# A four-layer graph network on one core: GpSimd waits for its own gathers ahead of every twelfth group

## The chip, the core and the metric

The program runs on one core of a Trainium2 chip. The metric is the device time of one execution in microseconds (us), the median over runs. The engines are TensorE (PE, with its weight loads PEld), VectorE (DVE), ScalarE (ACT), GpSimd (POOL) and SyncE (SP), each with a queue of its own; they meet on semaphores. Stores and plain loads are issued by SP, gathers by GpSimd.

## What is computed

Four graph layers in a row over the same graph of 3125 nodes and 100000 edges that are sorted by their target `dst`, each behind a layer norm and a rectifier, each added to its input `x`. The change touches the attention over incoming edges, which layer 1 does twice and layer 2 once:

```python
def _transformer_conv(x, src, dst, ...):       # layer 1, twice
    q = (x @ qw + qb).reshape(N, HEADS, CH)    # 8 heads of 16
    k = (x @ kw + kb).reshape(N, HEADS, CH)
    v = (x @ vw + vb).reshape(N, HEADS, CH)
    alpha = jnp.sum(q[dst] * k[src], axis=-1) * SCALE
    m = segment_max(alpha, dst); a = exp(alpha - m[dst])
    a = a / segment_sum(a, dst)[dst]
    out = segment_sum(v[src] * a[:, :, None], dst)
    return out + x @ sw + sb
# layer 2: the same with a bias by edge type, then projection, norms and a small MLP
# layer 0: two convolutions with the mean over edges; layer 3: two with the maximum over edges
```

## The kernel before

The edges lie in 128 partitions, 784 consecutive edges each, so the running sums and maxima over the edges of one target are scans along the free axis. Passes 0 and 1 (sums) go by another method. Passes 2, 3 and 4 are the attention passes, passes 5 and 6 the maxima; each walks the 784 steps in 56 groups of `GROUP` = 14 steps. The passes run one after the other, as each needs the node rows that the one before leaves.

For one group of an attention pass GpSimd issues 14 indirect DMAs. Each gathers, for the 128 edges of one step (one in each partition), the row of the source node out of `table[k]` in HBM: key and value, 256 numbers of 4 bytes, so 131 KB a gather. They land in one of `RING` = 3 slots of the buffer `ring` (which lies in `arena`) and count on the semaphore of the slot, `s_land` ("rows_landed"). Ahead of a group g from 3 on GpSimd waits on `s_att`, until VectorE has read the values of group g - 3 out of the slot. In groups 5, 12, 19, 26, ... (g mod 7 is 5) GpSimd first issues one more indirect DMA, `fetch_window`, for the queries of seven later groups.

VectorE works on group g in two parts. `part_a`: L1085 (queries of late edges), L1113 (moves the window on), then a wait until the 14 gathers of the group have landed, and L1092 (query times key), L1094 (sum to scores), L1097, L1099, L1101 (running maximum and exponents). `part_b`, one group behind: L1131, L1136 (value times weight), L1140 (the running sum, 4.15 us). ScalarE does the exponentials, spreads the queries, and lays the finished rows out in `outs` (L1579, L1582), which SP stores to HBM (L2183, 1.0 MB a group). At the end of a pass GpSimd joins the partitions' first rows (a gather of the head row, a scatter of it at L2405 and a wait for that scatter) and gathers the rows of the nodes.

All gathers are recorded at L2316, in the helper `fetch`. Within GpSimd's queue the instructions go in the order in which they are written in `run_pass`; nothing reorders them.

Of the kernel before, what the change touches and what calls it, by code (L numbers as in the profile page):

```python
# [48 lines left out]
RING = 3  # L49
# [9 lines left out]
PICKED = (GROUPS - PICK_FROM) * MAKE  # L59
TURN_AT = 12  # L60
SHARE = 7
QROWS = SHARE + 1
SPANS = GROUPS // SHARE
MOVES = SHARE - 1
STEPS = GROUP * GROUPS
# [113 lines left out]
def gnn_kernel(nc, A):  # L179
# [10 lines left out]
    with ctx:  # L190
# [3 lines left out]
        def sem(name):  # L194
            return ctx.enter_context(nc.semaphore(name))
# [19 lines left out]
        WINDOW_AT = RING * GROUP * 2 * D  # L215
        arena = sb("arena", [P, WINDOW_AT + 2 * QROWS * D])
        ring = arena[:, 0:RING * GROUP * 2 * D].rearrange("p (s j w) -> p s j w", s=RING, j=GROUP)

        window = arena[:, WINDOW_AT:WINDOW_AT + 2 * QROWS * D].rearrange("p (s r f) -> p s r f", s=2, r=QROWS)

# [250 lines left out]
        s_land = [sem(f"rows_landed{s}") for s in range(RING)]  # L471
# [113 lines left out]
        def landed(k, g):  # L585
            return land_count[k, g]
# [4 lines left out]
        def window_moved(k, g):  # L591

            return att_number(k) * (MOVES * SPANS) + g // SHARE * MOVES + g % SHARE

# [26 lines left out]
        def after_b(k, g, i):  # L621
            if isinstance(g, int) and g == GROUPS - 2:
                return (GROUPS - 1) * A_STEPS[k] + 1 + B_STEPS * g + att_base[k] + i
            na = GROUPS if isinstance(g, int) and g == GROUPS - 1 else g + 2
            return na * A_STEPS[k] + B_STEPS * g + att_base[k] + i
# [43 lines left out]
        def _(v):  # L669
# [436 lines left out]
            def move_on(k, g):  # L1106

                if g % SHARE == 0:
                    return
                rows3, left, n = window[:, g // SHARE % 2, :, :], QROWS - g % SHARE, window_moved(k, g)  # L1110
                if n > 1:
# [1182 lines left out]
        def _(pool):  # L2294
# [41 lines left out]
            def run_pass(k):  # L2336
# [21 lines left out]
                with pool.Else():  # L2358
                    fetch_window(k, 0)
                    for g in range(GROUPS):  # L2360
                        s, first = g % RING, g * GROUP
                        if g >= RING:
                            pool.wait_ge(s_att, after_b(k, g - RING, 2))
                        if g % SHARE == SHARE - 2 and g + 2 < GROUPS:
                            fetch_window(k, (g + 2) // SHARE)
                        for j in range(GROUP):
                            fetch(ring[:, s, j, :], table[k], src_i[:, first + j:first + j + 1], s_land[s])
# [111 lines left out]
```

## Time and profile before

| what | us |
|---|---|
| median of 3 runs | 5820.93 |
| lowest and highest run | 5820.36, 5821.15 |
| span of the profiled execution | 6562.2 |
| attention pass 2, first gather to last L1092 | 780 to 1865 |
| attention pass 3 | 1960 to 3045 |
| attention pass 4 | 3154 to 4242 |
| maximum passes 5 and 6, first to last scan of each | 4408 to 5416, 5502 to 6498 |

The profiled execution is the only one of which the trace tells; no time of it besides its span is given, and that span is 741 us above the median of the runs. All moments in this text are us from the start of that span. In the timeline a row is one instruction with its start, its duration, and in brackets how long its engine stood idle before it and what ended that; "issue" means that the profile shows nothing that it waited for. The duration of an indirect DMA on POOL is the time in which GpSimd makes it, and not the time until its data have landed.

### The profile page before, as it was taken

The page shows a single profiled execution, that of the slowest core. Times are in us where ns is not written, and L with a number is a line of the kernel's source. Part 1 is how long each engine was busy: PE and PEld are TensorE (multiplying, and loading weights), DVE is VectorE, ACT ScalarE, POOL GpSimd, SP SyncE. Part 2 cuts the span into 40 slices and gives each one's busy share as a digit, 9 for nine tenths or more (in the row PEclk, how much of TensorE's full clock was granted, in tenths as well). Part 3 has the DMA queues.
Part 4 walks back from the last instruction along what each step waited for, and adds up shares of the span by engine and source line. Part 5 has one row for each costly group of instructions (what it writes and reads, how often), then busy time and mean ns, then how long its engine had stood idle before and what let it go on. Part 6 is the DMA issues. An engine that isn't in the chain of part 4 may idle for free.

```text
span 6562.2 us, 44574 instructions
## 1 busy us (share of the span) xinstructions
PE 2310.6 (35%) x14635; PEld 1387.8 (21%) x14635; DVE 4507.3 (69%) x5353; ACT 2519.0 (38%) x3136; POOL 3944.3 (60%) x3878
## 2 busy tenths in 40 slices
PE   4988400000020000000100000046877783778886
PEld 2775300000000000000000000023444441444443
DVE  7978587777767777776787777764655653656654
ACT  2330144444424444443344444433444442444443
POOL 1001377777747777775677777656665555566664
PEclk8998755555555555555555555567888895889887
DMA  2233354444434444443454444412333322333332
GB/s 64 83 136 135 110 163 152 153 147 146 152 117 151 157 148 147 152 148 113 134 160 152 147 148 146 142 46 86 102 110 101 101 95 73 102 110 109 98 103 84
DMA packets 257146, 807.72 MB, mean 123 GB/s; under 512 B 72026, under 2 KB 108938, under 8 KB 253123
## 3 DMA queue, kind: packets, MB, share of 16 engines
q0 software_dynamic: 162688, 416.67, 22.2%
q1 hardware_dynamic: 94279, 389.14, 16.2%
q8 instruction: 54, 0.88, 0.1%
q14 instruction: 125, 1.02, 0.0%
HBM read 473.23 MB, written 332.30 MB: 123 GB/s over the span
## 4 chain that ended last, share of the span: by engine, by line
POOL 38%; PE 26%; issue 22%; DVE 8%; ACT 2%; another core or an unknown queue 2%; DMA 1%; SPq 0%; DVEq 0%; POOLq 0%; ACTq 0%
POOL arena L2316 38%; PE pair_ps L1864 20%; PE pair_ps L1966 3%; DVE outs L917 2%; ACT outs L1702 1%; PE banks_ps L1830 1%; PE banks_ps L1942 1%; DVE outs L995 1%; PE pair_ps L1873 0%; DVE bn_st L700 0%; DVE H L1048 0%; ACT arena L1680 0%; PE pair_ps L1982 0%; PE banks_ps L1807 0%
## 5 line engine op out<-in xcount | busy, mean ns | idle before, releaser
L2316 POOL DMA_INDIRECT arena<-table,src_i x3596 | 3684.6, 1025 | 1549.8 <-issue 1134.4
L1842 PE MATMUL pair_ps<-ident,tails 128*128 128x128 f32 x9 | 2.7, 439 | 3331.7 <-DVE tails L1246 3331.7
L1864 PE MATMUL pair_ps<-bias,arena 128*128 128x384 bf16 x4050 | 803.9, 348 | 279.9 <-issue 239.9
L1092 DVE TENSOR_TENSOR pair_ps<-pair_ps,arena 128x1792 f32<-128x1792 f32 x168 | 341.5, 2033 | 764.7 <-DMA arena<-table,src_i 589.1
L1864 PE MATMUL pair_ps<-work,arena 128*128 128x384 bf16 x4050 | 760.5, 338 | 206.4 <-issue 204.8
L995 DVE TENSOR_TENSOR_SCAN outs<-arena,banks_ps 128x1920 f32<-128x1920 f32 x112 | 465.2, 4153 | 494.3 <-ACT banks_ps L1688 446.2
L1842 PEld LDWEIGHTS pair_ps<-ident,tails 128*128 128x128 f32 x9 | 1.5, 213 | 3334.0 <-DVE tails L1246 3334.0
L1140 DVE TENSOR_TENSOR_SCAN work<-work,banks_ps 128x1920 f32<-128x1920 f32 x168 | 697.7, 4153 | 5.8
L1562 ACT ACTIVATE LD<-DE 128x112 f32<-128x112 f32 x168 | 49.8, 296 | 1440.9 <-issue 571.3
L1864 PEld LDWEIGHTS pair_ps<-bias,arena 128*128 128x128 bf16 x4050 | 406.9, 102 | 661.6 <-issue 452.8
L1582 ACT COPY outs<-work 128x1792 f32<-128x1792 f32 x171 | 541.0, 3165 | 0.0
L1702 ACT COPY outs<-outs 128x1792 f32<-128x1792 f32 (+1 forms) x114 | 370.1, 3249 | 429.0 <-issue 336.0
L1864 PEld LDWEIGHTS pair_ps<-work,arena 128*128 128x128 bf16 x4050 | 399.4, 100 | 536.6 <-issue 311.5
L2316 POOL DMA_INDIRECT H<-slot_sums,rden x50 | 49.3, 986 | 586.2 <-DMA slot_sums<-H 571.6
L1085 DVE COPY_PREDICATED pair_ps<-late,pair_ps 128x1792 f32<-128x1792 uint8 x168 | 340.7, 2028 | 25.1 <-ACT pair_ps L1604 10.2
L1136 DVE TENSOR_TENSOR banks_ps<-arena,banks_ps 128x1792 f32<-128x1792 f32 x168 | 340.8, 2028 | 5.8
L1094 DVE TENSOR_REDUCE UA<-pair_ps 128x112 f32<-128x1792 f32 x168 | 340.3, 2026 | 5.8
L1012 DVE TENSOR_TENSOR bias<-arena,KEEP 128x640 bf16<-128x640 bf16 x810 | 338.3, 492 | 3.3 <-ACT arena L1709 3.3
L1012 DVE TENSOR_TENSOR work<-arena,KEEP 128x640 bf16<-128x640 bf16 x810 | 336.9, 490 | 0.0
L1687 ACT COPY banks_ps<-pair_ps 128x384 f32<-128x384 f32 x108 | 49.8, 461 | 729.3 <-remote 397.5
L1004 DVE COPY bias<-pair_ps 128x384 f32<-128x384 f32 x108 | 58.7, 543 | 373.9 <-remote 347.2
L1966 PE MATMUL pair_ps<-arena 128*128 128x320 bf16 (+1 forms) x1875 | 281.5, 303 | 6.3 <-DVE arena L1032 6.1
(321 smaller groups left out, 4353.4 us busy)
## 6 DMA issues: line engine op xcount, KB each, us to landing
rows_att<-outs SPq DMA_DIRECT2D x165, 1008.0 KB
rows_plain<-outs SPq DMA_DIRECT2D x110, 896.0 KB
arena<-table,src_i POOLq DMA_INDIRECT x3596
kept_counts<-arena SPq DMA_DIRECT2D x15, 2000.0 KB, 6.4
bias<-sources SPq DMA_DIRECT2D x108, 192.0 KB
arena<-kept_counts SPq DMA_DIRECT2D x10, 2000.0 KB, 8.3
outs<-kept_counts SPq DMA_DIRECT2D x5, 2000.0 KB, 8.0
table<-arena SPq DMA_DIRECT2D x18, 512.0 KB, 3.0
```

The costliest lines, as they stand in the source:

```text
L995: v.tensor_tensor_scan(sums_plain, decay_plain, msg, 0.0, ALU.add, ALU.max).then_inc(s_agg, 1)
L1012: ins = v.tensor_tensor(hot_made[u, g % 2][:, t0:t1, :], pick_tile[:, g % 2, MAKE - 1 - u, :].unsqueeze(1).to_broadcast([P, PIECE, P]), ti ...
L1085: chain(v.copy_predicated(prod, late[:, first:first + GROUP].unsqueeze(2).to_broadcast(wide), next_q.unsqueeze(1).to_broadcast(wide)))
L1092: chain(v.tensor_tensor(prod, prod, ring[:, s, :, 0:D], ALU.mult))
L1094: chain(v.tensor_reduce(scores, prod.rearrange("p j (h c) -> p j h c", c=CH), AX.X, ALU.add))
L1136: chain(v.tensor_tensor(by_edge(msg).rearrange("p j (h c) -> p j h c", c=CH), vals, wts, ALU.mult))
L1140: chain(v.tensor_tensor_scan(OS[b], dB[b], msg, 0.0, ALU.mult, ALU.add))
L1582: act.copy(out_att[:, b, j0:j1, 0:D], by_edge(OS[b])[:, j0:j1, :]).then_inc(s_rows, 1)
L1702: act.copy(out_plain[:, j0:j1, :], by_edge(sums_plain)[:, j0:j1, :]).then_inc(s_rows, 1)
L1864: ins = pe.matmul(picked_ps[g % 2], parts3[:, a, t, :], hots_made[g % 2][:, :, t, :], start=t == a == 0, stop=t == NB - 1 and a == 2)
L1966: ins = pe.matmul(product_ps(k, b)[:, 0:n], parts3[:, a, t, :], counts[:, t, 0:n], start=i == 0, stop=i == total - 1)
L2316: pool.indirect_dma_start(dst, None, tab, bass.IndirectOffsetOnAxis(ap=idx, axis=0))\
```

## The change

Ahead of the groups 12, 24, 36 and 48 of each of the three attention passes GpSimd waits until all gathers of the group before have landed, on the semaphore of that group's slot. It is in the branch that runs for these inputs (the other one is for graphs in which a group spans many targets).

```diff
 SHARE = 7
+PAUSE = 12
...
                         s, first = g % RING, g * GROUP
                         if g >= RING:
                             pool.wait_ge(s_att, after_b(k, g - RING, 2))
+                        if g and g % PAUSE == 0:
+                            pool.wait_ge(s_land[(g - 1) % RING], landed(k, g - 1))
                         if g % SHARE == SHARE - 2 and g + 2 < GROUPS:
                             fetch_window(k, (g + 2) // SHARE)
                         for j in range(GROUP):
```

`landed(k, g)` is the count that the slot's semaphore has when all 14 gathers of group g are there (16 for each gather). No instruction changes its place. On GpSimd's queue, from the last group before the wait (group 11 of pass 2) to the first gather of group 13, there stands before:

```order
L2316 DMA arena<-table,src_i 128x256 [waits att_steps]
L2316 DMA arena<-table,src_i 128x256 x13
L2316 DMA arena<-qtable,dst_i 128x1024 [waits att_steps]
L2316 DMA arena<-table,src_i 128x256 x14
L2316 DMA arena<-table,src_i 128x256 [waits att_steps]
```

and with the change (two lines were added above, so the helper is at L2317):

```order
L2317 DMA arena<-table,src_i 128x256 [waits att_steps]
L2317 DMA arena<-table,src_i 128x256 x13
L2317 DMA arena<-qtable,dst_i 128x1024 [waits rows_landed2,att_steps]
L2317 DMA arena<-table,src_i 128x256 x14
L2317 DMA arena<-table,src_i 128x256 [waits att_steps]
```

Nothing moved; the first indirect DMA of group 12 (here the window fetch) waits for the landing of group 11's rows besides the ring slot. At groups 24, 36 and 48 it is the group's first gather that has both waits.

## Rows read from the trace of the kernel before

**Rows 1.** The page: busy time of the engines, chain that ended last.

```profile
PE 2310.6 (35%) x14635; PEld 1387.8 (21%) x14635; DVE 4507.3 (69%) x5353; ACT 2519.0 (38%) x3136; POOL 3944.3 (60%) x3878
...
POOL 38%; PE 26%; issue 22%; DVE 8%; ACT 2%; another core or an unknown queue 2%; DMA 1%; SPq 0%; DVEq 0%; POOLq 0%; ACTq 0%
```

**Rows 2.** Groups of instructions, DVE, 779:1864; count | busy, mean ns | idle before.

```profile
L1092 DVE TENSOR_TENSOR pair_ps<-pair_ps,arena 128x1792 f32<-128x1792 f32 x55 | 111.8, 2033 | 261.1 <-DMA arena<-table,src_i 211.8 <-issue 49.3
```

**Rows 3.** Waits of POOL, 1100:1860: total, times, longest us.

```profile
POOL arena L2316 <- issue: 184.9, 543, 0.9
```

**Rows 4.** Timeline of POOL and DVE, groups 11 to 13, and the pass's first gather.

```profile
779.74 0.95 POOL L2316 DMA_INDIRECT arena<-table,src_i  x1 [0.30 <-issue]
...
991.90 0.96 POOL L2316 DMA_INDIRECT arena<-table,src_i  x1 [0.30 <-issue]
...
993.17 0.95 POOL L2316 DMA_INDIRECT arena<-table,src_i  x1 [0.30 <-issue]
...
995.91 2.03 DVE L1092 TENSOR_TENSOR pair_ps<-pair_ps,arena 128x1792 f32<-128x1792 f32 x1 [2.99 <-DMA arena<-table,src_i]
...
1009.96 0.45 DVE L1113 COPY_PREDICATED arena<-next_on,arena 128x256 f32<-128x256 uint8 x1
...
1012.06 0.96 POOL L2316 DMA_INDIRECT arena<-table,src_i  x1 [0.31 <-issue]
...
1017.12 2.03 DVE L1092 TENSOR_TENSOR pair_ps<-pair_ps,arena 128x1792 f32<-128x1792 f32 x1 [6.71 <-DMA arena<-table,src_i]
```

**Rows 5.** Timeline at group 5's end; then L1092 in 892:1000, its idle time.

```profile
886.95 0.96 POOL L2316 DMA_INDIRECT arena<-table,src_i  x1 [0.30 <-issue]
...
891.83 2.03 DVE L1092 TENSOR_TENSOR pair_ps<-pair_ps,arena 128x1792 f32<-128x1792 f32 x1 [6.50 <-issue]
...
  DMA arena<-table,src_i: 15.4, 6
```

**Rows 6.** Timeline of POOL between passes 2 and 3.

```profile
1887.04 0.95 POOL L2316 DMA_INDIRECT head<-rows_att,head_i  x1 [26.12 <-DVE tails L1165]
1892.57 1.01 POOL L2405 DMA_INDIRECT rows_att<-head,head_i  x1 [4.58 <-DVE head L1195]
1895.18 0.97 POOL L2316 DMA_INDIRECT arena<-rows_att,last_i  x1 [1.60 <-DMA rows_att<-head,head_i]
```

**Rows 7.** L2316 over the whole span: start to landing, where it is known.

```profile
DMA to landing us min/median/max: 2.5/2.5/2.6
```

**Rows 8.** L2316 on POOL in stretches: us, busy (count), clock, DMA share, GB/s; then 779:1030.

```profile
850.00:1000.00 150.00, 113.75 (x120) 0.50 0.53 168
1300.00:1450.00 150.00, 115.52 (x107) 0.50 0.46 149
2030.00:2180.00 150.00, 113.44 (x121) 0.50 0.53 171
2600.00:2750.00 150.00, 112.95 (x108) 0.50 0.46 152
...
L2316 POOL DMA_INDIRECT arena<-table,src_i x196: 952/957/1775, 779.7 to 1029.8; - x196
L2316 POOL DMA_INDIRECT arena<-qtable,dst_i x3: 950/952/952, 778.5 to 994.4; - x3
```

**Rows 9.** Timeline of groups 15 and 16, and group 55's first gather.

```profile
1068.55 0.96 POOL L2316 DMA_INDIRECT arena<-table,src_i  x1 [0.30 <-issue]
...
1071.33 2.03 DVE L1092 TENSOR_TENSOR pair_ps<-pair_ps,arena 128x1792 f32<-128x1792 f32 x1 [2.75 <-DMA arena<-table,src_i]
...
1080.74 1.08 POOL L2316 DMA_INDIRECT arena<-table,src_i  x1 [0.30 <-issue]
1082.13 1.09 POOL L2316 DMA_INDIRECT arena<-table,src_i  x1 [0.30 <-issue]
...
1087.73 1.10 POOL L2316 DMA_INDIRECT arena<-table,src_i  x1 [0.30 <-issue]
...
1092.42 2.03 DVE L1092 TENSOR_TENSOR pair_ps<-pair_ps,arena 128x1792 f32<-128x1792 f32 x1 [6.16 <-DMA arena<-table,src_i]
...
1840.93 1.09 POOL L2316 DMA_INDIRECT arena<-table,src_i  x1 [0.30 <-issue]
```

**Rows 10.** Waits in passes 5 and 6, 4391:6547.

```profile
PE pair_ps L1864 <- issue: 444.8, 527, 3.0
```

## The prediction, made before the change was run

> **What bounds the kernel now.** I read the busy row and the chain that ended last first: GpSimd (POOL) is busy 60% of the span and its line L2316, the indirect DMA of every gather, holds 38% of the chain, with 22% more under "issue", which is for a large part the 0.30 us between two gathers [rows 1]. The change touches the attention passes alone (passes 2, 3 and 4), so what matters is which wait ends last in them. In pass 2 VectorE stands idle before L1092, the first step that needs the gathered rows, for 261.1 us in 55 groups, 4.75 us a group, most of it put down to the gathers [rows 2]. GpSimd waits for nobody there: all of its idle time from 1100 to 1860 us is "issue", the longest piece 0.9 us [rows 3], though every group from the fourth on has a wait for VectorE (a free ring slot) in its code. So GpSimd issues without a pause, VectorE follows 2.7 us behind, and a microsecond added on GpSimd is a microsecond added to the pass.
>
> The rates of the two say how firm this is. A gather starts every 1.26 us in the first part of a pass (991.90, 993.17) [rows 4], so a group of 14 takes 17.6 us, and 18.9 us where a window fetch goes ahead of it (every seventh group); the mean is 17.8. VectorE's own work on a group runs from 995.91 to 1010.41 us without a hole, 14.5 us, and 15.1 us with the longest form of L1113 (about 1.0 us in place of 0.45) [rows 4]. GpSimd would have to get down to 1.04 to 1.08 us a gather before VectorE set the pace.
>
> **The change part by part.** It adds 12 waits: groups 12, 24, 36 and 48 of three passes. No instruction, DMA or queue entry is added or moved, since the wait is laid on the instruction that waits for VectorE already. Behind each on GpSimd's queue stand the group's 14 gathers (at group 12 the window fetch too, whose rows ScalarE needs two groups later); VectorE at L1092 waits for the last of them, and all of GpSimd's later groups move along. The ring's three slots don't help, because GpSimd is never ahead by more than the gathers in flight.
>
> Cost of one pause: without it the next DMA starts 1.26 us after the last gather's start. With it, it starts when that gather has landed and the wait is released. Three rows bound that from the same kernel. (a) GpSimd itself waits for a DMA of its own once a pass: the scatter of the head row starts at 1892.57 and the gather that waits for it at 1895.18, 2.61 us later [rows 6]: a loss of 1.35 us. (b) VectorE's release by the last gather of group 11, in the place of the first pause: gather at 993.17, L1092 at 995.91, 2.74 us [rows 4]: a loss of 1.48 us. (c) Where the store of a finished group (1.0 MB, queued by SP) runs just then, the landing is late: last gather of group 12 at 1012.06, L1092 at 1017.12, 5.06 us [rows 4]: a loss of 3.80 us. In the undisturbed part of pass 2 this befell the groups with a window fetch ahead of them, group 5 (886.95 to 891.83, 4.88 us) and group 12: the longer group pushes its last gathers under the store. Groups 6 to 11 landed as in (b), with 15.4 us of idle time on VectorE before L1092 for the six [rows 5]. Of the groups 11, 23, 35 and 47 whose landing is awaited, 47 alone is of that kind (47 mod 7 is 5). So a pass costs 3 x 1.48 + 3.80 = 8.2 us and three passes 24.7 us. The bounds are 12 x 1.35 = 16 us (no store in the way) and 12 x 3.80 = 46 us (a store each time). I take 24.7, as that is the pattern of the part in which nothing else holds the gathers up.
>
> The Trainium skill, "DMA: Bandwidth & Descriptors" (section Anatomy of one DMA — SWDGE (gpsimd) path), has a rule that speaks against such a wait: a DMA from GpSimd costs about 2.0 us that do not depend on its size, mostly the receipt of the last write, and issuing on hides it. For the 131 KB of a gather its fit gives an estimate of 2.3 us, which with the 1.26 us taken off and the release of about 0.3 us makes 1.3 us a pause, 16 us in all. The trace has 2.5 us from start to landing [rows 7], so the measured number is used.
>
> **The second rate, and what could be gained.** From about group 14 of each pass to its end the gathers come slower: 120 in 150 us (1.25 us) from 850 us on, 107 in 150 us (1.40 us) from 1300 us on, and in pass 3 the same [rows 8]. Gathers of that stretch start about 1.40 us apart (1080.74, 1082.13) [rows 9]. Whether the timed executions have this too, and whether a pause at group 12, just before the slow stretch, can end it, decides between two stories. Two things speak against a gain. First, it looks like an allowance that runs out: a pass starts fast after a time with few gathers, issues 199 indirect DMAs in the 251 us from 778.5 to 1029.8 [rows 8], where 1.40 us each would allow 179, and then goes at the allowance's rate. By that, a pause of 1.5 to 3.8 us gives back one to three gathers' worth and no more: it would be paid back (cost near zero) and not reset. Second, the profiled execution is 741 us longer than the timed ones, and the slow stretches look like part of that. TensorE in the last two passes shows the same sort of hole, matmuls held back with "issue" as the only reason, for 444.8 us in all [rows 10]. In pass 2 the groups take 19.3 us on the mean (first gather of group 0 at 779.74, of group 55 at 1840.93 us) [rows 4, 9]; at 17.8 us each pass would be 82 us shorter, 247 us for three; 247 + 445 = 692 us, near the 741. If GpSimd ran so fast in the timed executions that VectorE set the pace, its 4.75 us of waiting a group would go, 3 x 55 x 4.75 = 784 us, more than the whole difference by itself. So I take 1.26 us without slow stretches for the timed executions.
>
> The Trainium skill, "NOTIFIC — the notification-queue block" (section 7.1), says that the block which writes the profiler's records holds its producers back when its internal pipeline fills. By that rule the 1.40 us belongs to the profiled execution alone, and the timed cost is the full 24.7 us. No run here shows it yet.
>
> **The rivals.** (1) Nothing measurable, by two roads. VectorE sets the pace in the timed executions: from 1.08 us a gather down, GpSimd waits for a slot anyway, and the pause disappears in that wait. Or the 1.40 us is real and the pauses are paid back as above. Both give 0 to 5 us: 5821 to 5826. For it: 741 us of difference whose place I only infer. Against it: [rows 3] and the sum above. (2) Slower than forecast: a store is in the way of most awaited landings, as in much of the slow stretch: there group 15 landed in time (1068.55 to 1071.33) and group 16 did not (1087.73 to 1092.42, 4.69 us) [rows 9], and so on in turns. Cost 30 to 46 us: 5851 to 5867. It decides if the store of a group falls on the last gathers of groups 23 and 35 too. (3) Faster: the slow stretch is real in the timed executions and is a state of the gathers' queue that an empty queue clears. Then 42 groups of each pass go from 19.6 to 17.8 us: 3 x 42 x 1.8 = 227 us, less the 25 us of the waits: about 5620. It decides if the first gathers after a pause, with nothing in flight, start a new fast stretch of ten groups and more. For it: the slow part begins at the same place in all three passes, after a time of rest. Against it: the rests that went before were 26 us and longer (26.12 us ahead of pass 3's first DMA of the head) [rows 6]. (4) The wait does nothing because the gathers have landed already. That can't be on these rows: the wait comes 1.26 us after a gather that takes 2.5 us to land.
>
> **How the numbers follow.** The profile's span can't serve as the base of the time; the cost is in absolute microseconds on the path and is added to the median of the runs, 5820.93 + 24.7 = 5845.6 us. Forecast (15 to 30 us): 0.58. Rival 2: 0.12. Rival 1: 0.21. Rival 3: 0.09. A difference of 0.2%, 11.6 us, is about what a measurement of this kernel can tell from none, so slower is 0.58 + 0.12 = 0.70, same 0.21, faster 0.09. The range leaves out rival 3 and the upper end of rival 2: 5820 to 5858.
>
> **What the profile of the changed kernel would show.** Right: at twelve places GpSimd stands idle 1.6 to 4.1 us before a gather (or the window fetch), with the landed rows as the releaser, VectorE's idle time before L1092 is longer by as much one group later, and elsewhere the gathers are still 1.26 us apart in the first groups. The span itself may grow by less, as slow stretches can pay a pause back there. Rival 3: rows at 1.26 us for many groups after a pause, and a span shorter by hundreds of microseconds. Rival 1: a timed difference under 11 us, and, if by the first road, no trace of it in the profile. What would make me wrong is mainly the pace of GpSimd in an execution without the profiler, which no row shows.

## The result, and the profile after

The changed kernel takes 5859.4 us (median of 4 runs, 5855.97 to 5862.95), the kernel before 5820.65 us beside it (4 runs, 5817.55 to 5821.15). The ratio is 1.0067, with a 95% interval of 1.0053 to 1.0081: **slower by 38.75 us**. The prediction was 5845.6 us, so the sign and the mechanism held, and the 24.7 us for it were too few; the time lies 1.4 us above the range. On other chips the executions of one kernel lie in two bands some 30 to 40 us apart (the kernel before at 5810 to 5815 and at 5842 to 5863 us on one chip), most of it in passes 5 and 6, which take 771 to 776 us each in the profiles of shorter executions, 780 to 790 us in those of longer ones, and 776 and 779 us here.

The page of the changed kernel, busy row and chain of work that ended last, to set against [rows 1]:

```profile
span 5859.4 us, 44586 instructions
PE 2146.4 (37%) x14635; PEld 1381.6 (24%) x14635; DVE 4505.2 (77%) x5353; ACT 2524.1 (43%) x3136; POOL 3729.2 (64%) x3878
...
POOL 59%; issue 20%; DVE 9%; PE 7%; DMA 3%; ACT 1%; SPq 0%; DVEq 0%; POOLq 0%
```

This execution ran as long as the timed ones. POOL now has 59% of the chain, and PE 7% in place of 26%: the holes of [rows 10] are not there. The waits of POOL over the whole span (waited for: total us, times, longest) show the change itself, which [rows 3] had nothing of:

```profile
POOL arena L2317 <- DMA arena<-table,src_i: 22.7, 9, 2.5
POOL arena L2317 <- DVE pair_ps L1093: 18.8, 3, 6.7
```

Twelve waits, as many as there are pauses: nine of 2.5 us and three of 5.4 to 6.7 us. Gathers are otherwise 0.30 us apart, so the waits themselves add 22.7 + 18.8 - 12 x 0.30 = **37.9 us** to GpSimd's queue, against 38.75 us measured (31 to 47 us by the interval). All the lost time is there.

A pause of the first kind, ahead of group 24 of pass 2 (timeline of POOL and DVE; start, duration, what; in brackets the idle time before it and what ended it):

```profile
1197.79 0.96 POOL L2317 DMA_INDIRECT arena<-table,src_i  x1 [0.30 <-issue]
1200.56 2.03 DVE L1093 TENSOR_TENSOR pair_ps<-pair_ps,arena 128x1792 f32<-128x1792 f32 x1 [2.73 <-DMA arena<-table,src_i]
1201.27 0.96 POOL L2317 DMA_INDIRECT arena<-table,src_i  x1 [2.52 <-DMA arena<-table,src_i]
```

The last gather of the group starts at 1197.79, its landing releases VectorE at 1200.56, 2.77 us later (2.74 in [rows 4]), and GpSimd's wait ends in the same moment. But its next gather starts only at 1201.27, **0.71 us behind the release**. The trace has the landing wait itself too, an instruction on GpSimd's queue (how often, duration in ns, first and last start):

```profile
L2366 POOLq EVENT_SEMAPHORE  x12: 17/17/17, 983.3 to 3856.5; - x12
```

In all twelve places it passes within 0.01 us of the start of L1093, so that start can be read as the release. One of the second kind, ahead of group 48, with SP's issue of a store:

```profile
1632.85 0.95 POOL L2317 DMA_INDIRECT arena<-table,src_i  x1 [0.30 <-issue]
...
1633.07 0.32 SPq L2184 DMA_DIRECT2D rows_att<-outs  x1
...
1637.70 2.03 DVE L1093 TENSOR_TENSOR pair_ps<-pair_ps,arena 128x1792 f32<-128x1792 f32 x1 [6.42 <-DMA arena<-table,src_i]
1639.77 2.02 DVE L1095 TENSOR_REDUCE UA<-pair_ps 128x112 f32<-128x1792 f32 x1
...
1640.48 0.95 POOL L2317 DMA_INDIRECT arena<-table,src_i  x1 [6.68 <-DVE pair_ps L1093]
```

The landing is late, 4.85 us (predicted from group 12: 5.06), and then the next gather starts **2.78 us behind the release**. The trace names L1093 as releaser, since the gather starts 0.75 us after that instruction's end; whether it is the cause is a question for the experiments. The program now has 44586 instructions in place of 44574: the landing wait, which was expected to be laid on the gather, is an instruction of its own on GpSimd (the gather itself carries the wait for VectorE's count).

### The profile page after: what moved, and what is told of

Its sections match the earlier page's. It is cut to its first block, busy times and chain, and to the rows that moved or that the text cites. A ratio compares the mean times of both kernels' runs of the same rounds, so it can differ in the third digit from the quotient of the medians.

```text
span 5859.4 us, 44586 instructions
## 1 busy us (share of the span) xinstructions
PE 2146.4 (37%) x14635; PEld 1381.6 (24%) x14635; DVE 4505.2 (77%) x5353; ACT 2524.1 (43%) x3136; POOL 3729.2 (64%) x3878
## 3 DMA queue, kind: packets, MB, share of 16 engines
q0 software_dynamic: 162688, 416.67, 24.7%
## 4 chain that ended last, share of the span: by engine, by line
POOL 59%; issue 20%; DVE 9%; PE 7%; DMA 3%; ACT 1%; SPq 0%; DVEq 0%; POOLq 0%
POOL arena L2317 59%; PE pair_ps L1967 4%; DVE outs L918 2%; DMA arena<-table,src_i 1%; DVE work L1141 1%; PE banks_ps L1831 1%; PE banks_ps L1943 1%; POOL H L2317 1%; DVE pair_ps L1093 0%; DVE banks_ps L1137 0%; DVE H L1049 0%; PE pair_ps L1983 0%; DVE bias L1049 0%; DVE UA L1095 0%; PE banks_ps L1808 0%
## 5 line engine op out<-in xcount | busy, mean ns | idle before, releaser
L2317 POOL DMA_INDIRECT arena<-table,src_i x3596 | 3470.2, 965 | 1136.6 <-issue 1091.5
L1093 DVE TENSOR_TENSOR pair_ps<-pair_ps,arena 128x1792 f32<-128x1792 f32 x168 | 341.5, 2033 | 563.7 <-DMA arena<-table,src_i 563.5
L1865 PE MATMUL pair_ps<-bias,arena 128*128 128x384 bf16 x4050 | 689.0, 330 | 38.3 <-DVE bias L1013 38.3
L1865 PE MATMUL pair_ps<-work,arena 128*128 128x384 bf16 x4050 | 694.2, 332 | 0.0
L2317 POOL DMA_INDIRECT H<-slot_sums,rden x50 | 49.7, 994 | 582.2 <-DMA slot_sums<-H 567.6
L1095 DVE TENSOR_REDUCE UA<-pair_ps 128x112 f32<-128x1792 f32 x168 | 340.3, 2026 | 5.8
L1685 ACT COPY banks_ps<-arena 128x1408 f32<-128x1408 f32 (+1 forms) x112 | 151.0, 1348 | 343.3 <-DMA arena<-table,src_i 343.3
L1564 ACT ACTIVATE work<-DE 128x1792 f32<-128x1792 f32 x168 | 282.5, 1682 | 0.0
```

The lines of the kernel that those rows point to most:

```text
L1093: chain(v.tensor_tensor(prod, prod, ring[:, s, :, 0:D], ALU.mult))
L1095: chain(v.tensor_reduce(scores, prod.rearrange("p j (h c) -> p j h c", c=CH), AX.X, ALU.add))
L1865: ins = pe.matmul(picked_ps[g % 2], parts3[:, a, t, :], hots_made[g % 2][:, :, t, :], start=t == a == 0, stop=t == NB - 1 and a == 2)
L2317: pool.indirect_dma_start(dst, None, tab, bass.IndirectOffsetOnAxis(ap=idx, axis=0))\
```

## The experiments

All kernels are set against the kernel before. Where a run was timed, the ratio stands with its interval, which is 8 to 22 us to either side. The length of the attention passes in the trace is the finer measure: from the first to the last L1092 (L1093) of passes 2, 3 and 4. In the kernel before, profiled again, these are 985.7 + 980.0 + 991.5 = 2957.2 us. "By the waits" is the sum of GpSimd's idle times at the pauses, less 0.30 each. The waits are the finer of the two: a longer execution shows a little in the attention passes as well. In e7, which has no pause in them and was profiled in such an execution, they are 3.4 us longer than in the kernel before; e2, e4, after_again, f1 and f2 were too, and their passes are 2 to 6 us over the waits. (In l1 the window fetches are moved too, so the passes differ by more than the waits. The kernels f0, e7 and e8 have sections of their own.)

| run | pauses | timed ratio [95%] | passes 2 to 4, us more | by the waits |
|---|---|---|---|---|
| the change | 12, 24, 36, 48 | 1.0067 [1.0053, 1.0081] | 38.2 | 37.9 |
| e1_only12 | 12 | 0.9986 [0.9949, 1.0023] | 5.6 | 6.6 |
| e2_only48 | 48 | 1.0015 [0.9976, 1.0053] | 20.4 | 17.8 |
| e3_swapped | the four, landing wait first | 1.0026 [0.9988, 1.0064] | 27.0 | 29.4 |
| e5_long_landed | the four, wait long fulfilled | 0.9976 [0.9937, 1.0015] | -0.2 | 0 |
| e4_after_window | 13, 20, 27, 41 | 1.0133 [1.0117, 1.0149] | 77.0 | 73.3 |
| after_again | the change once more | 1.0070 [1.0056, 1.0084] | 43.5 | 37.7 |
| f3_fifty | 12, 24, 36, 50 | 1.0046 [1.0030, 1.0063] | 27.8 | 26.6 |
| f1_mult_done | 12, 24, 36, for L1093's end | 1.0066 [1.0049, 1.0083] | 42.3 | 38.6 |
| f2_reduce_done | 12, 24, 36, for L1095's end | 1.0099 [1.0082, 1.0116] | 59.5 | 57.3 |
| h1_mult_mixed | 13, 24, 36, 41, for L1093's end | one run | 73.2 | 74.2 |
| h2_with_nop | 13, 24, 36, 41, an empty instruction more | one run | 49.2 | 49.0 |
| h3_two_later | in 13, 20, 27, 41, two gathers later | one run | 11.5 | 11.2 |
| k2_one_later | in 13, 20, 27, 41, one gather later | one run | 27.7 | 26.1 |
| k1_store_held | 13, 20, 27, 41, store held back | one run | 51.0 | 51.4 |
| l1_window_later | 13, 28, 41, 49, window fetch moved | one run | 42.9 | 50.7 |

### Was the slow rate of the first profile real?

The kernel before, profiled once more, with nothing changed:

> The kernel before, profiled once more. If the slow stretches of the first profile (1.40 us a gather, holes of TensorE, a span 741 us over the timed one) belonged to that execution alone, the span is 5810 to 5860 us, 118 gathers start in 150 us everywhere in an attention pass, and VectorE's idle time ahead of its multiplication is as in the kernel with pauses of no cost, some 560 us. If the waits of the change removed them, the slow stretches are there again and the span is over 6000 us.

It took 5813.0 us, its span is 5811.3 us, and the gathers on POOL in three stretches of pass 2 (us, busy (count), clock, DMA share, GB/s) are:

```profile
core 0 of [0], span 5811.3 us
850.00:1000.00 150.00, 113.75 (x120) 0.50 0.52 164
1010.00:1160.00 150.00, 114.04 (x119) 0.50 0.51 162
1300.00:1450.00 150.00, 113.75 (x120) 0.50 0.50 162
```

119 or 120 gathers everywhere, where [rows 8] had 107 from 1300 us on. The wait of TensorE with 444.8 us [rows 10] is gone too. So the 1.40 us a gather and the 741 us belonged to that one profiled execution of the kernel before, not to the kernel, and the waits of the change had nothing to clear away. VectorE's idle time ahead of L1092 in pass 2, here and then in the changed kernel (count | busy, mean ns | idle):

```profile
L1092 DVE TENSOR_TENSOR pair_ps<-pair_ps,arena 128x1792 f32<-128x1792 f32 x55 | 111.8, 2032 | 182.0 <-DMA arena<-table,src_i 182.0
```

```profile
L1093 DVE TENSOR_TENSOR pair_ps<-pair_ps,arena 128x1792 f32<-128x1792 f32 x55 | 111.8, 2033 | 196.0 <-DMA arena<-table,src_i 196.0
```

182.0 us in place of the 261.1 of [rows 2], and 14.0 us more with the pauses, and pass 2 became 14.3 us longer (1000.0 against 985.7). VectorE takes the pauses over one to one.

### Does GpSimd set the pace?

```diff
-                so_far[group % RING] += 16 * (GROUP - picks(pass_k, group))
+                so_far[group % RING] += 16 * (GROUP - picks(pass_k, group) - (KINDS[pass_k] == ATT))
...
-                        for j in range(GROUP):
+                        for j in range(GROUP - 1):
```

(Here the last of the 14 gathers of each attention group is left out, with the counts of the landing semaphore to match; the rows of that step are old ones.)

> The kernel before with 13 gathers in place of 14 in each group of the attention passes (the rows of the last step of a group are left out, and the last slot place keeps old rows); VectorE's and ScalarE's work is the same. If GpSimd sets the pace at 1.26 us a gather: 168 x 1.26 = 212 us less, 5609 us. If VectorE sets it, or nearly: its work of 14.5 to 15.1 us a group stays, and the time falls by much less than that, to 5750 us or more.

5636.09 us, a ratio of 0.9631 [0.9618, 0.9644]. The attention passes became 919.3, 912.5 and 920.0 us long: 205.4 us less for 168 gathers left out, 1.22 us each. All but 0.04 us of the 1.26 us of a gather is on the path. A group of 13 takes 16.4 us, still above the 14.5 to 15.1 us of VectorE's own work [rows 4]. This is the strongest support for the first step of the prediction.

### Waiting or the instruction?

```diff
-                            pool.wait_ge(s_land[(g - 1) % RING], landed(k, g - 1))
+                            pool.wait_ge(s_land[(g - 1) % RING], landed(k, g - 1) - 16 * GROUP)
```

> All twelve waits, but for the count that the slot's semaphore had one round of the ring earlier, so they wait for rows that landed some 50 us before. It leaves the instruction and takes the waiting away. Waiting theory: no cost, 5820 to 5822 us. Rival (a second wait on the queue itself keeps GpSimd from making the next DMA ready ahead): 12 x 0.4 = 5 us or more, 5826 us.

The wait asks for a count that was reached three groups before. The attention passes are 0.2 us shorter than without it. The instruction costs nothing; standing idle until the landing does.

### One pause at a time

```diff
-                        if g and g % PAUSE == 0:
+                        if g == PAUSE:         # e1_only12
+                        if g == 4 * PAUSE:     # e2_only48
```

> The wait stands ahead of group 12 alone, once in each of the three attention passes; groups 24, 36 and 48 have none. Account theory (each pause costs GpSimd's idle time before the next DMA less 0.30 us, and nothing comes back): the changed kernel's trace has 2.52 us of idle time there, so 3 x 2.22 = 6.7 us over the kernel before, about 5827 us. Rival (one pause shifts the stores against the gathers for the rest of the pass, and that shift is the cost): most of the 39 us are there with the first pause already, 5840 us or more.

> The wait stands ahead of group 48 alone, once in each attention pass. Account theory: idle time before it is 6.68, 6.70 and 5.40 us in the changed kernel's trace, less 0.30 each 17.9 us, about 5839 us, nearly half of the whole loss from a quarter of the waits. Rival (every pause costs the same 39 / 12 = 3.2 us): 9.7 us, 5830 us.

In this pair the timed ratios can't tell 5 from 20 us, and neither is told from 1. The traces do: three pauses at group 12 idle 2.56, 2.46 and 2.53 us and lengthen the passes by 5.6 us; three at group 48 idle 6.62, 6.60 and 5.44 us and lengthen them by 20.4 us (17.8 us by the waits). Each is within 0.1 us as long as in the changed kernel, so the pauses don't act on each other, and nothing is paid back.

### Which pauses are dear

```diff
-                        if g and g % PAUSE == 0:
+                        if g in (13, 20, 27, 41):      # e4_after_window
+                        if g in (12, 24, 36, 50):      # f3_fifty
```

> Four waits a pass as in the change, but ahead of groups 13, 20, 27 and 41, each right behind a group with a window fetch (12, 19, 26, 40), whose last rows land under a store. Store theory (a landing under a store costs 5.4 to 6.7 us of idle time, as at group 48): 12 x 6.0 = 72 us, about 5893 us. Rival (group 48 is dear by its place near the end of the pass and not by the window fetch): 12 x 2.2 = 27 us, 5847 us.

> The pauses stand ahead of groups 12, 24, 36 and 50 instead of 12, 24, 36 and 48 (k of the four is the same, and so is the place near the pass's end). Theory A (what makes group 48 dear is that the last gather ahead of it is issued as the store that follows the window's fetch runs; group 50 has no such store): the idle time ahead of the next gather is 2.5 us at all 12 pauses, a pass of attention is 4 x 2.2 = 8.9 us longer than without pauses, 26.6 us in all; measured beside the kernel before, 1.0046. Theory B (the pass's end makes it dear, since the buffers behind it are the last three): group 50 costs 6 us or more like 48, 12 x 2.2 + 3 x 3.8 = 38 us in all, 1.0066.

Ahead of group 50 in place of 48 GpSimd idles 2.5 us as ahead of the other three, and the whole 5843.14 us against 5815.42, 27.7 us. Four pauses behind groups with a window fetch idle 5.4 to 7.2 us each and cost 77 us in all, twice the change itself for the same number of waits. So it is not the end of the pass that makes a pause dear. It is the group with 15 indirect DMAs ahead of it.

### The order of the two waits

```diff
+                        if g and g % PAUSE == 0:
+                            pool.wait_ge(s_land[(g - 1) % RING], landed(k, g - 1))
                         if g >= RING:
                             pool.wait_ge(s_att, after_b(k, g - RING, 2))
-                        if g and g % PAUSE == 0:
-                            pool.wait_ge(s_land[(g - 1) % RING], landed(k, g - 1))
```

> All twelve waits, but written ahead of the wait for VectorE, so that the wait for the landing is laid on the DMA itself and the one for VectorE stands on an instruction of its own before it. In the changed kernel the wait for the landing has an instruction of its own, and the DMA behind it starts 0.72 us after it passes (nine times) or 2.78 us (three times, at group 48); the DMA that waits for the scatter by itself starts about 0.3 us after the landing. If the second instruction is the price: 0.4 us less at each pause, 5 us in all, 5854 us; and if the 2.06 us more at group 48 are the DMA's own wait for VectorE passing late (it starts 0.73 us after the end of L1093), these go too, another 6 us, 5848 us. If GpSimd needs these times to start again after a rest, whatever it waited for: as the changed kernel, 5859 us.

POOL and DVE at group 12, then at group 48:

```profile
979.89 2.03 DVE L1093 TENSOR_TENSOR pair_ps<-pair_ps,arena 128x1792 f32<-128x1792 f32 x1 [3.01 <-DMA arena<-table,src_i]
980.12 0.95 POOL L2317 DMA_INDIRECT arena<-qtable,dst_i  x1 [2.06 <-DMA arena<-table,src_i]
...
1632.37 2.03 DVE L1093 TENSOR_TENSOR pair_ps<-pair_ps,arena 128x1792 f32<-128x1792 f32 x1 [6.50 <-DMA arena<-table,src_i]
1633.82 0.95 POOL L2317 DMA_INDIRECT arena<-table,src_i  x1 [5.35 <-issue]
```

With this order the restart is 0.23 us in place of 0.72 at the nine plain pauses and 1.45 in place of 2.78 at the three dear ones, and the passes are 27.0 us longer than before, not 38. So it matters on which of the two the landing wait is laid: 8.5 us of the 37.9 by the waits (29.4 here). The second of these rows also shows that L1093 is not what holds GpSimd, as the trace's releaser had it: the gather starts 0.58 us before L1093 ends.

### Where the late restart comes from

The first two idle longer by choice: GpSimd waits for VectorE's work on the group ahead, not for the landing.

```diff
-                        if g and g % PAUSE == 0:
-                            pool.wait_ge(s_land[(g - 1) % RING], landed(k, g - 1))
+                        if g in (12, 24, 36):
+                            pool.wait_ge(s_att, after_a(k, g - 1, 2))   # f1: L1093 has ended
+                            pool.wait_ge(s_att, after_a(k, g - 1, 3))   # f2: L1095 has ended
```

> Ahead of groups 12, 24 and 36 of an attention pass GpSimd waits not for the landing but for the end of VectorE's multiplication of the group ahead, 0.36 + 2.03 us later; VectorE starts its sum of 2.02 us at that same moment. Group 48 has no pause. Theory A (a long wait of GpSimd and a 2 us instruction of VectorE that starts with the release together make the next gather 2.06 us later): idle 1.45 + 0.36 + 2.06 + 2.78 = 6.7 us at each of nine pauses, 9 x 6.4 = 57 us in all. Theory B (what costs the 2.06 us is that the landing came under a store, in the queues that GpSimd uses; here none is late): idle 1.45 + 0.36 + 2.06 + 0.72 = 4.6 us, 9 x 4.3 = 39 us in all.

> As f1_mult_done, but GpSimd waits for the end of VectorE's sum, another 2.06 us later, when VectorE starts a scan of 0.41 us and then instructions of 0.3 to 0.4 us. Theory A (long wait and a 2 us instruction of VectorE together): the next gather has no 2 us instruction ahead of it, so idle 1.45 + 0.36 + 2.06 + 2.06 + 0.72 = 6.65 us (up to 0.4 more if the scan holds it), 9 x 6.4 = 57 us in all, as much as f1 although the wait is 2.06 us longer. Theory C (a long wait alone makes the restart 2.78 us): idle 8.7 us, 9 x 8.4 = 76 us in all. Theory B (late landing under a store): 6.65 us, 57 us, with f1 at 39.

f1 at group 24:

```profile
1204.44 2.03 DVE L1093 TENSOR_TENSOR pair_ps<-pair_ps,arena 128x1792 f32<-128x1792 f32 x1 [2.69 <-DMA arena<-table,src_i]
1206.51 2.02 DVE L1095 TENSOR_REDUCE UA<-pair_ps 128x112 f32<-128x1792 f32 x1
...
1207.22 0.95 POOL L2317 DMA_INDIRECT arena<-table,src_i  x1 [4.58 <-DVE pair_ps L1093]
```

Release at 1206.51, gather at 1207.22: 0.71 us, with GpSimd idle for 3.9 us before and a 2.02 us instruction of VectorE starting in the same moment. f2 idles 5.9 us before its release, and the gather follows 0.72 us behind it (idle 6.60 to 6.75 us in all). Neither a long idle time nor VectorE's start makes the 2.78 us. Both came out at the numbers of theory B: 38.75 and 59.3 us timed, 38.6 and 57.3 us by the waits.

The next two set pauses of both kinds into one kernel, with other instructions at the pause.

```diff
-                        if g and g % PAUSE == 0:
+                        if g in (13, 24, 36, 41):
-                            pool.wait_ge(s_land[(g - 1) % RING], landed(k, g - 1))
+                            pool.wait_ge(s_att, after_a(k, g - 1, 2))   # h1
+                            pool.wait_ge(s_land[(g - 1) % RING], landed(k, g - 1))   # h2
+                            pool.nop(nofuse=True)                                    # h2
```

> Pauses ahead of groups 13 and 41 (behind a window's store, where a landing wait cost 6.6 us) and of 24 and 36 (plain, 2.5 us), each waiting for the end of VectorE's multiplication of the group ahead instead of the landing. Plain ones as in f1_mult_done: 4.6 us idle. At 13 and 41: theory A (whatever releases GpSimd there, its next gather starts 2.78 us later, since the extra 2.06 us belongs to the restart behind a late landing) gives 3.5 + 0.36 + 2.06 + 2.78 = 8.7 us; theory B (with the landing wait GpSimd is in truth held until that multiplication has ended, so waiting for its end adds nothing) gives 6.65 us, as with the landing wait; 5.4 us in the last attention pass, where the store holds less.

> The landing wait at the same four groups with one empty instruction of GpSimd behind it. Writing the landing wait on the gather itself instead of on an instruction of its own had moved the restart from 0.72 to 0.23 us at plain pauses and from 2.78 to 1.45 us at late ones. Theory A (behind a late landing every instruction that GpSimd's sequencer handles is 0.8 to 1.3 us dearer, as when they must be fetched anew): idle at 24 and 36 3.0 us, at 13 and 41 7.5 to 8 us (5.4 + 0.8 to 1.3 in the last pass). Theory B (GpSimd is held until the multiplication has ended): 3.0 and 7.1 us, or 6.65 where the empty instruction is hidden in that wait.

h1 at group 13:

```profile
1004.96 2.03 DVE L1093 TENSOR_TENSOR pair_ps<-pair_ps,arena 128x1792 f32<-128x1792 f32 x1 [6.36 <-DMA arena<-table,src_i]
1007.02 2.03 DVE L1095 TENSOR_REDUCE UA<-pair_ps 128x112 f32<-128x1792 f32 x1
...
1009.80 0.95 POOL L2317 DMA_INDIRECT arena<-table,src_i  x1 [8.70 <-DVE UA L1100]
```

The release moved by 2.06 us and the gather with it: again 2.78 us behind (1007.02 to 1009.80), and the releaser named is now another instruction that happened to end there. At groups 24 and 36 it is 0.71 us in the same kernel. So GpSimd isn't held until the multiplication has ended; the delay belongs to the restart at that group. One rival is left by h1: here too a 2.03 us instruction of VectorE (L1095) starts with the release, and the gather follows 0.75 us behind its end, as it does behind L1093's in the change. That GpSimd is held by whatever long instruction VectorE has just begun is against e3, where the gather starts before L1093 has ended, and against l1 below. In h2 the empty instruction is not seen at all: 2.5 us at 24 and 36, where both theories had 3.0, and 6.6 at 13 and 41 (5.40 and 5.55 in pass 4). The extra doesn't go by the number of instructions.

Then the same landing, awaited one or two gathers later, and the store taken away from it:

```diff
                         for j in range(GROUP):
+                            if j == 2 and g in (13, 20, 27, 41):    # h3; k2: j == 1
+                                pool.wait_ge(s_land[(g - 1) % RING], landed(k, g - 1))
```

```diff
                             sp.wait_ge(s_rows, rows_base[k] + 2 * (g + 1) + half)
+                            if g in (10, 17, 24, 38):               # k1, pauses as in e4
+                                sp.wait_ge(s_land[(g + 2) % RING], landed(k, g + 2))
```

> At groups 13, 20, 27 and 41 the landing wait stands not ahead of the group but ahead of its third gather, 2.5 us later in GpSimd's order, so that GpSimd stands idle for about 1.0 us before the same late landing instead of 3.5. Theory A (the 2.06 us belongs to a long idle time of GpSimd ahead of the release, over about 2 us): idle 1.0 + 0.36 + 0.72 = 2.1 us. Theory B (it belongs to the late landing and to VectorE's multiplication, which starts with it): 1.0 + 0.36 + 2.78 = 4.1 us. Two more gathers are then ahead of the wait only in GpSimd's order; the landing of the group ahead is not moved.

> The landing wait of e4_after_window one gather later: ahead of the second gather of groups 13, 20, 27 and 41. GpSimd then stands idle for some 2.6 us ahead of the release, between the 1.3 us of h3_two_later (restart 0.24 us) and the 3.9 us of e3_swapped (restart 1.45 us, the wait written on the gather in both); in the last attention pass some 1.4 us. Theory A (the extra belongs to an idle time of over about 2 us behind a landing under a store): restart 1.45 us in passes 2 and 3 and 0.24 in pass 4. Theory B (it belongs to the first gather of a group, which also waits for VectorE's count): restart 0.24 us in all.

> Pauses ahead of groups 13, 20, 27 and 41 as in e4_after_window, where each left GpSimd idle for 6.6 us (5.5 in the last attention pass) and restarted it 2.78 us after the release. Here the store that used to run under the last gather (rows of groups 10, 17, 24 and 38) is held back by SyncE until that gather has landed. Theory A (the store makes both the late landing and the late restart): idle 1.45 + 0.36 + 0.72 = 2.5 us. Theory B (the store makes the landing late, but the restart of 2.78 us belongs to these groups for another reason, such as the window's gather one group earlier): 1.45 + 0.36 + 2.78 = 4.6 us.

k2 at group 13 (pause ahead of its second gather), then k1 (pause ahead of its first, store held back):

```profile
1001.71 0.95 POOL L2317 DMA_INDIRECT arena<-table,src_i  x1 [0.30 <-issue]
1005.46 0.95 POOL L2317 DMA_INDIRECT arena<-table,src_i  x1 [2.81 <-DMA arena<-table,src_i]
...
1005.23 2.03 DVE L1093 TENSOR_TENSOR pair_ps<-pair_ps,arena 128x1792 f32<-128x1792 f32 x1 [6.35 <-DMA arena<-table,src_i]
```

```profile
1000.67 0.96 POOL L2319 DMA_INDIRECT arena<-table,src_i  x1 [0.30 <-issue]
1006.22 0.95 POOL L2319 DMA_INDIRECT arena<-table,src_i  x1 [4.59 <-DVE pair_ps L1093]
...
1003.43 2.03 DVE L1093 TENSOR_TENSOR pair_ps<-pair_ps,arena 128x1792 f32<-128x1792 f32 x1 [4.37 <-DMA arena<-table,src_i]
```

In k2 GpSimd is released 0.23 us before its gather, with 2.6 us of idle time ahead (1.4 to 1.6 us in pass 4), and so in all twelve places. In h3 it is 0.24 us, with 1.3 us of idle time (1.55 to 1.70 us in all in passes 2 and 3, under theory A's 2.1, since the wait sits on the gather here; in pass 4 the landing has all but come and the gap is 0.36 to 0.46 us). Behind the same late landing the late restart is gone. In k1 the landing is no longer late: 2.76 us (1000.67 to 1003.43) where e4 had 4.82. So the store does make the landing late, at 2.06 us a pause. But the next gather is still 2.79 us behind the release, though GpSimd was idle for 1.8 us until then, no longer than at a plain pause; so its idle time isn't why either. **The late landing and the late restart are two different things**, which until here always came together. The store makes the first and not the second, which belongs to the first gather of the group.

Last, the window fetch itself was moved one group later:

```diff
-                        if g % SHARE == SHARE - 2 and g + 2 < GROUPS:
-                            fetch_window(k, (g + 2) // SHARE)
+                        if g % SHARE == SHARE - 1 and g + 1 < GROUPS:
+                            fetch_window(k, (g + 1) // SHARE)
-                        if g and g % PAUSE == 0:
+                        if g in (13, 28, 41, 49):
```

> GpSimd's gather of the next window (128 rows of 4 KB) is moved one group later, from groups 5, 12, 19, ... to groups 6, 13, 20, ..., and the pauses stand ahead of groups 13, 28, 41 and 49. Theory A (the restart of 2.78 us belongs to the first gather behind a group that holds a window's gather): ahead of 28 and 49 release to next gather is 2.78 us, ahead of 13 and 41 (whose group ahead now has none) 0.72 us. Theory B (it belongs to the place in the program, groups 6 behind a multiple of 7, whatever GpSimd fetched): 2.78 us ahead of 13 and 41, 0.72 ahead of 28 and 49. How long each landing takes may differ, since the stores stand at the same places and the gathers of those groups one place earlier or later.

Groups 13 and 28 of pass 2:

```profile
999.01 0.95 POOL L2317 DMA_INDIRECT arena<-table,src_i  x1 [0.30 <-issue]
1002.50 0.95 POOL L2317 DMA_INDIRECT arena<-qtable,dst_i  x1 [2.53 <-DMA arena<-table,src_i]
...
1269.99 0.95 POOL L2317 DMA_INDIRECT arena<-table,src_i  x1 [0.30 <-issue]
1277.54 0.95 POOL L2317 DMA_INDIRECT arena<-table,src_i  x1 [6.59 <-DVE pair_ps L1093]
...
1274.83 2.03 DVE L1093 TENSOR_TENSOR pair_ps<-pair_ps,arena 128x1792 f32<-128x1792 f32 x1 [6.95 <-DMA arena<-table,src_i]
```

Group 13, always dear so far, idles 2.53 us now, and group 28 6.59 us, with the gather 2.71 us behind L1093's start. Here VectorE starts 0.07 us late: GpSimd's own landing wait passes at 1274.76, and from there it is 2.78 us as everywhere. So the gather keeps its distance from GpSimd's release and not from VectorE's instruction, behind whose end it starts by 0.68 us in place of 0.75. Group 49 does as 28 (5.47 to 6.67 us). Group 41 is plain but for 0.45 us (2.97 to 3.07 us, restart 1.17), which nothing here explains. All three passes show the same. (The first indirect DMA behind the pause is the window's own gather at 13 and 41, as at group 12 of the change.) The dear pause moves with the window's gather, as theory A had it: not a place in the program, but that gather in the group ahead, makes the restart late, and the longer group also pushes its last gathers under the store. Whether it is its rows of 4 KB or only that it is one DMA more, no run separates. Why GpSimd needs 2 us more at the first gather of the next group if it has been made to wait there, and nothing if it hasn't (the gaps there are 0.30 us in the kernel before), no run shows. It stays open.

### Other passes

The same pauses in the maximum passes 5 and 6 and none in the attention passes:

```diff
                     for g in range(GROUPS):
                         if g >= RING:
                             pool.wait_ge(s_spread, scanned(k, g - RING))
+                        if g and g % PAUSE == 0:
+                            pool.wait_ge(s_land[(g - 1) % RING], landed(k, g - 1))
```

> No wait in the attention passes; the same wait ahead of every twelfth group of the two maximum passes (5 and 6) in its place, eight in all. There GpSimd has 11 gathers a group and waits for ScalarE's reading of the ring slot in most groups. If a pause costs only where GpSimd sets the pace: 0 to 2 us, 5821 to 5823 us. If a pause costs its idle time wherever it stands: 8 x 2.2 = 18 us, 5838 us.

1.0062 [1.0049, 1.0076], 35 us (5885.14 against 5850.31), far more than I had thought these passes would show. The eight pauses idle 2.2 to 5.5 us, 28.5 us in all by the waits, 6 us less than the time, which is within its interval. One of them, ahead of group 24 of pass 5 (last gather, next gather):

```profile
4464.51 0.95 POOL L2317 DMA_INDIRECT arena<-table,src_i  x1 [0.30 <-issue]
4469.96 0.95 POOL L2317 DMA_INDIRECT arena<-table,src_i  x1 [4.50 <-DMA arena<-table,src_i]
```

GpSimd's wait passes at 4469.25: the landing is late, 4.74 us, and the restart is 0.71 us. Five of the eight landings take 4.2 to 5.8 us, and the restart is 0.71 to 0.72 us at all eight. These passes have no window fetch, so this is the case that k1 lacks, a late landing without a late restart. The trace says who pays (last lines of the view of L2317, and of L2316 in the kernel before: who waited for it):

```profile
  ACT banks_ps L1685: 397.4, 97
```

```profile
  ACT banks_ps L1684: 331.3, 88
```

ScalarE waits for the gathers in 88 of 112 groups of these passes in the kernel before as well. GpSimd's gathers set the pace there too, which TensorE's and VectorE's high shares hide on the page.

The change itself, run once more on the same chip:

> The changed kernel itself beside these, on the same chip. 12 pauses by the account: 9 x 2.22 + 17.9 = 37.9 us over the kernel before, about 5859 us.

5888.38 against 5850.31 us, 1.0070: the same ratio at another level. Its twelve waits are 2.46 to 2.61 us (nine) and 6.54, 6.64 and 5.38 us.

## Why the prediction was wrong by 14 us, point by point

- **GpSimd sets the pace, a microsecond added there is one added to the pass.** Right: e8 (1.22 us a gather left out), and the account by the waits, which comes within 2 us of the timed differences of f3, f1, f2 and the change (27.7 for 26.6, 38.75 for 38.6, 59.3 for 57.3, 38.75 for 37.9). That is closer than their intervals of 8 to 10 us to either side allow to claim; single runs lie up to 6 us off (k2, 32.4 for 26.1).
- **No instruction is added, the wait is laid on the one that waits for VectorE.** Wrong: 12 are added, and the landing wait stands on them. As instructions they cost nothing (e5), but with the landing wait on the gather the restarts would have been 8.5 us shorter (e3).
- **The cost of a plain pause, 1.48 us.** Wrong, the first of two terms that were too small. The step took VectorE's release, 2.74 us behind the last gather, for the moment of GpSimd's next gather. The landing was right (2.77 us at group 24); left out was the restart, 0.72 us from the release to the gather. A plain pause costs 2.2 us. Row (a), GpSimd's own wait for the scatter [rows 6], has a restart in it (the gather starts 0.26 us behind the scatter's landing), but that wait sits on the gather itself, as in e3 where it is 0.23 us.
- **Group 48, 3.80 us.** The late landing was foreseen from group 12, with the right reason (k1) and nearly the right size (4.85 for 5.06 us). The restart of 2.78 us wasn't, the second term; like the first it stood at nothing, without a reason. A pause there costs 6.4 us, 5.1 in pass 4 where the store holds the landing less.
- **The sum.** The two omissions make 9 x 0.72 + 3 x 2.78 = 14.8 us; 24.7 + 14.8 = 39.5 us, and 1.6 us less for landings that came a little earlier, in pass 4 above all, makes the 37.9 us by the waits. That is the whole miss. The idle time at a pause, forecast at 1.6 to 4.1 us, is 2.5 to 6.7 us.
- **Which pauses meet the store.** Right: group 48 alone (f3, e4). Rival 2, which had stores in the way elsewhere too, reached the right time for a wrong reason: nine pauses had none. The upper bound of 46 us held the truth, and the range was cut off below it because that rival's upper end was the part to be left out. But rows (b) and (c), from which the bounds came, have no restart of GpSimd in them, so even 46 us was no upper bound: e4, twelve waits as well, cost 73 us by the waits.
- **The slow stretches and the holes of TensorE belong to the profiled execution alone.** Right, as f0 shows directly; rival 3 and one road of rival 1, which rested on them, fall. The other road of rival 1, VectorE setting the pace, falls with e8. "NOTIFIC — the notification-queue block" of the Trainium skill (section 7.1) says that the writer of the profiler's records holds back its producers when it is full. The runs agree with that so far as the same kernel was profiled at 6562.2 and at 5811.3 us; that the records were the cause, none of them shows.

## What to carry to other kernels

Where an engine issues DMAs back to back and sets the pace, a wait for its own DMAs costs the landing plus a restart less one issue interval, here 2.77 + 0.72 - 1.26 = 2.2 us, and each part has to be read from the engine that waits, not from another that the same landing releases. Make such a wait, if it must be, away from groups with an extra gather or a store under way (2.2 us, against 4.3 with the extra gather alone in k1 and 6.4 with both), and as the last condition on the DMA itself. If a profiled execution is 13% longer than the timed ones, profile it again before reasoning about its rates.

## What the runs showed of the hardware

- An indirect DMA of GpSimd starts 0.72 us behind the release of a wait that is an instruction of its own (the change, f1, f2, e7), and 0.23 us behind one that sits on the DMA (e3, k2, h3). It doesn't depend on how long GpSimd was idle until then (1.8 to 5.9 us in the first case, 1.3 to 2.7 us in the second).
- The first indirect DMA of a group whose predecessor held a gather of 128 rows of 4 KB starts 2.78 us behind the release (1.45 if the wait sits on it), though without a wait it follows at the usual 0.30 us. The delay moves with that gather; its cause is open.
- A 1.0 MB store that starts 0.2 us behind the last gather's start delays that gather's landing from 2.76 to 4.8 us; one that starts 1.4 us behind it (SP's issue ahead of group 24) does it no harm. A late landing alone doesn't make the restart late (e7).
- The releaser that the trace names is the last event before the start. At the dear pauses it named VectorE's L1093, and in h1 L1100, neither of which it was held by: the gather starts a fixed 2.78 us behind GpSimd's own release, and they had ended shortly before.
